# An attention and expert layer on one core: a new order of the step, with the combine weights spread by DMA

## The chip, the cores and the metric

One core of a Trainium2 chip runs the whole layer. The metric is device time in microseconds from the start to the end of one execution.

## The reference

Sixteen sequences ("batches" below) of 256 tokens with 128 features pass through attention and then an expert layer, each with a residual:

```python
x = x + attn(layernorm(x), Wqg, Wkv, Wout)
x = x + ffn(layernorm(x), ...)
# attn, per head (16 heads, 16 key and 64 value features)
q, k, v = l2norm(q), l2norm(k), l2norm(v)
attn = square(relu(q @ k.T)); aggr = attn @ v
out = tanh(norm(aggr)) * aggr / norm(aggr) * tanh(silu(gates)) @ Wout
# ffn, 16 routed experts (4 chosen per token, group limited) and one shared
inter = silu(x @ w_gate[e]) * (x @ w_up[e])
y = sum_e combine[:, e] * (inter[e] @ w_down[e]) + shared
```

`combine` holds the four chosen scores of a token, normed to a sum of 2.5, and zeros.

## The kernel before

The work is a software pipeline over batches. In step s (from -2 to 18) six stages run side by side on different batches: `L` (batch s+2: layer norm, transposed `xT`, projections `qk` and `v`), `P` (s+1: gate projection `g`, norms of q, k, v), `A` (s: scores, relu, square, values of 16 heads), `O` (s-1: head norms, output projection `y`, residual, second layer norm, `x2T`), `F` (s-2: router `lg`, nine gate and up projections `gu`, combine weights), `D` (s-3: down projection `y2`). Steps 2 to 15 hold `F` within the general plan; steps 16 and 17 have end plans of their own.

A step has eight slots. In each, TensorE runs the fillers that `FILL` lists for the slot, then the scores of the next pair of heads, then the values of this pair (`values` of slot k end the slot). Every engine follows this order in its own queue: ScalarE reads PSUM (relu, silu, squares, copies), GpSimd squares the relus into `p` (L363), and VectorE's list is written out by hand in its `step`, slot by slot. Fillers take the four PSUM banks `ps_f` in turn, so job n of a step waits until job n-4 has been read (`wait_for_bank`).

Names that matter: `scale_hidden` (L920) multiplies the hidden values `it` by the combine weights of two experts' columns; these stand in PSUM, where `cT` (transposes) and `cB` 0 to 3 (matmuls with the selection matrix `sel`, L454) spread them over the partitions. `rT` and `rB` do the same for head scales, read by `scale_heads` (L911). `gate_up` (L903) multiplies silu and up projection, reading the bank of a `gu`. `gated_heads` (L949) multiplies the values by the gates. `head_norm_roots` runs the Newton rounds for inverse roots (L696 to L698), `route_scores`, `route_groups` and `route_experts` choose the experts. `low_parts`, `sums`, `low_rows` and `output_rows` are VectorE's readers of `qk`, `v`'s squares, `x2T` and `y2`. GpSimd also scales the values by their norms (L381), in slots 4 to 7.

SyncE (SP) issues all DMAs from one queue, in this order in a step: store of the output, load of `x_res`, load of `x_in`, store of the q and k parts to DRAM (`qk_rows`, 1 MB), and twelve loads back in another layout (`qkt`, 2 MB), which are wanted at the end of the next step.

## Time and profile before

| | |
|---|---|
| median of three runs | 714.83 us (712.07 to 715.86) |
| the profiled execution | 712.51 us, of which the span of instructions 710.5 us |
| mean granted TensorE clock | 0.99 |
| TensorE busy | 665.4 us (94%) |
| VectorE, ScalarE, GpSimd busy | 478.0, 431.8, 352.1 us |
| DMA queue of SP | 60.26 MB, 57.3% of 16 engines |

TensorE's busy share is from modelled ends of pipelined matmuls; the distance between the starts of two jobs is the better measure of what a job takes. A bracket behind a timeline row gives idle time before it and what ended it. Times of a row count from the start of the span.

### The profile page before, as it was taken

The page shows a single profiled execution, that of the slowest core. Times are in us where ns is not written, and L with a number is a line of the kernel's source. Part 1 is how long each engine was busy: PE and PEld are TensorE (multiplying, and loading weights), DVE is VectorE, ACT ScalarE, POOL GpSimd, SP SyncE. Part 2 cuts the span into 40 slices and gives each one's busy share as a digit, 9 for nine tenths or more (in the row PEclk, how much of TensorE's full clock was granted, in tenths as well). Part 3 has the DMA queues.
Part 4 walks back from the last instruction along what each step waited for, and adds up shares of the span by engine and source line. Part 5 has one row for each costly group of instructions (what it writes and reads, how often), then busy time and mean ns, then how long its engine had stood idle before and what let it go on. Part 6 is the DMA issues. An engine that isn't in the chain of part 4 may idle for free.

```text
span 710.5 us, 15317 instructions
## 1 busy us (share of the span) xinstructions
PE 665.4 (94%) x5160; PEld 515.8 (73%) x5160; DVE 478.0 (67%) x1771; ACT 431.8 (61%) x986; POOL 352.1 (50%) x368
## 2 busy tenths in 40 slices
PE   3689899999999999999999999999999999999977
PEld 2455567787787777778777778778777877767677
DVE  5745558676767777676767767576876767566684
ACT  3768576756566766656676775656667565644312
POOL 3348574645546464645555564555546355464200
PEclk9899999999999999999999999999999999999999
DMA  9998948290937639191855819094672909300000
GB/s 254 136 142 137 119 103 103 78 117 28 138 46 125 77 91 104 62 124 26 134 68 102 100 61 133 10 144 58 113 81 78 113 27 136 37 16 2 8 1 16
DMA packets 72829, 61.24 MB, mean 86 GB/s; under 512 B 8624, under 2 KB 72496, under 8 KB 72752
## 3 DMA queue, kind: packets, MB, share of 16 engines
q1 hardware_dynamic: 72752, 60.26, 57.3%
q8 instruction: 42, 0.69, 0.5%
q14 instruction: 35, 0.29, 0.1%
HBM read 41.37 MB, written 18.87 MB: 85 GB/s over the span
## 4 chain that ended last, share of the span: by engine, by line
PE 69%; ACT 12%; DVE 9%; issue 7%; POOL 2%; DMA 1%; SPq 0%; DVEq 0%; ACTq 0%; POOLq 0%
PE ps_a L539 14%; PE ps_f L395 10%; PE ps_f L479 9%; PE ps_f L458 8%; PE ps_f L396 7%; PE ps_f L397 7%; PE ps_s L507 5%; ACT sq L605 3%; PE ps_f L437 3%; ACT v L602 3%; ACT r L641 3%; DVE it L920 2%; POOL p L363 2%; PE ps_f L454 2%; DVE big L911 2%
## 5 line engine op out<-in xcount | busy, mean ns | idle before, releaser
L363 POOL TENSOR_TENSOR p<-r 128x512 f32<-128x512 f32 x256 | 260.8, 1040 | 288.7 <-ACT r L641 253.5
L641 ACT ACTIVATE r<-ps_s 128x512 f32<-128x512 f32 x256 | 142.3, 621 | 84.3 <-PE ps_s L507 79.0
L539 PE MATMUL ps_a<-p,v 128*64 128x256 f32 x1024 | 147.1, 393 | 3.5 <-POOL p L363 2.5
L539 PEld LDWEIGHTS ps_a<-p,v 128*64 128x64 f32 x1024 | 64.7, 136 | 45.3 <-POOL p L363 7.7
L633 ACT ACTIVATE it<-ps_f 128x256 f32<-128x256 f32 x144 | 55.2, 383 | 65.3 <-PE ps_f L397 54.4
L949 DVE TENSOR_TENSOR big<-ps_a,wt 128x256 f32<-128x256 f32 x128 | 54.1, 422 | 58.9 <-ACT big L650 57.2
L903 DVE TENSOR_TENSOR it<-ps_f,it 128x256 f32<-128x256 f32 x144 | 58.3, 421 | 42.3 <-ACT it L633 41.2
L479 PE MATMUL ps_f<-wdown,it 128*128 128x128 f32 x576 | 69.4, 280 | 2.8 <-DVE it L920 2.8
L479 PEld LDWEIGHTS ps_f<-wdown,it 128*128 128x128 f32 x576 | 66.8, 195 | 4.2 <-DVE it L920 3.8
L381 POOL TENSOR_TENSOR v<-v,vs 128x512 f32<-128x512 f32 x64 | 67.7, 1060 | 3.5 <-DVE vs L821 3.5
L650 ACT ACTIVATE big<-ps_a 128x256 f32<-128x256 f32 x128 | 53.5, 418 | 25.5 <-PE ps_f L437 22.9
L507 PE MATMUL ps_s<-qkt 64*128 64x256 f32 x512 | 65.3, 330 | 1.4 <-ACT r L641 1.1
L458 PEld LDWEIGHTS ps_f<-wout,big 128*128 128x128 f32 x512 | 59.5, 192 | 6.6 <-issue 5.8
L458 PE MATMUL ps_f<-wout,big 128*128 128x128 f32 x512 | 63.5, 278 | 0.7 <-DVE big L911 0.7
L611 ACT ACTIVATE wt<-ps_f 128x512 f32<-128x512 f32 x64 | 38.3, 598 | 31.6 <-PE ps_f L397 30.1
L507 PEld LDWEIGHTS ps_s<-qkt 64*128 64x128 f32 x512 | 38.6, 184 | 24.1 <-issue 10.9
L787 DVE TENSOR_REDUCE norms_m<-sq 128x8 f32<-128x512 f32 x64 | 43.7, 683 | 15.0 <-ACT sq L605 15.0
L780 DVE TENSOR_TENSOR qk_parts<-ps_f,qk_parts 128x512 fp32r<-128x512 f32 x32 | 22.0, 691 | 41.4 <-ACT qk_sq L597 41.4
L395 PE MATMUL ps_f<-x2h,weg_hi 128*128 128x256 f32 x144 | 46.9, 326 | 2.3 <-DVE o_sb L928 1.3
L911 DVE TENSOR_TENSOR big<-ps_f,big 128x512 f32<-128x512 f32 x64 | 42.4, 685 | 5.7 <-PE ps_f L454 5.6
L602 ACT ACTIVATE v<-ps_f 128x512 f32<-128x512 f32 x64 | 42.2, 659 | 4.3 <-DVE sel L768 2.2
L920 DVE TENSOR_TENSOR it<-ps_f,it 128x512 f32<-128x512 f32 x64 | 43.4, 684 | 0.5
(154 smaller groups left out, 1444.5 us busy)
## 6 DMA issues: line engine op xcount, KB each, us to landing
qk_rows<-qk_parts SPq DMA_DIRECT2D x16, 1024.0 KB, 4.5
qkt<-qk_rows SPq DMA_DIRECT2D x64, 256.0 KB, 9.6
qkt<-qk_rows SPq DMA_DIRECT2D x128, 128.0 KB, 9.0
x_in<-in_L_attn_tokens SPq DMA_DIRECT2D x16, 128.0 KB, 2.2
x_res<-in_L_attn_tokens SPq DMA_DIRECT2D x16, 128.0 KB, 13.6
out<-o_sb SPq DMA_DIRECT2D x16, 128.0 KB, 13.6
big<-in_L_attn_Wqg SPq DMA_DIRECT2D x1, 640.0 KB, 4.1
big<-in_L_attn_Wkv SPq DMA_DIRECT2D x1, 640.0 KB, 5.3
```

What stands on the lines that cost most here:

```text
L363: pool.tensor_tensor(p[h % 4][:], r[h % 2][:], r[h % 2][:], ALU.mult).then_inc(probs_done, 1)
L381: pool.tensor_tensor(view, view, broadcast(scale, [P, NP, DV], 2), ALU.mult)\
L395: pe.matmul(dst, stat[0], mov[0], start=True, stop=False)
L458: last = pe.matmul(ps[:, 0:D], aw[pb][:, c, tok[j]], wout[:, c, :], start=(c == 0), stop=(c == NP - 1))
L479: last = pe.matmul(ps[:, 0:D], it[:, c, tok[j]], wdown[:, c, :], start=(c == 0), stop=(c == FC - 1))
L507: last = pe.matmul(ps_s[e][:, t * N:(t + 1) * N], qkt[q][rows, 1, k, t * P:(t + 1) * P], qkt[q][rows, 0, k, :], start=True, stop=True)
L539: last = pe.matmul(ps_a[64 * e:64 * e + 64, 0:N], v[s % 3][:, t, h * DV:(h + 1) * DV], p[h % 4][:, t * N:(t + 1) * N], start=(t == 0), sto ...
L602: act.activation(v[b % 3][:, j // 2, (j % 2) * 512:(j % 2 + 1) * 512], ps[:], ACT.Copy)
L641: act.activation(r[h % 2][:], ps_s[h % 2][:], ACT.Relu).then_inc(relu_done, 1)
L903: dve.tensor_tensor(it[:, c, :], bank[("gu", c)][:, N:2 * N], it[:, c, :], ALU.mult)\
L911: dve.tensor_tensor(part, bank[("rB", j)][:].rearrange("p (c n) -> p c n", n=N), part, ALU.mult)\
L920: dve.tensor_tensor(part, bank[("cB", j)][:].rearrange("p (c n) -> p c n", n=N), part, ALU.mult).then_inc(read["cB"], 1)
```

## The change

- `FILL` is new: `cB` and `cT` leave it, `cD` (two transposes of the 16 combine weights) comes in; `v` 3 moves to slot 0 of the next step (stage `P`); the two halves of `y2` stand in slots 0 and 1; `gu` runs in slots 2 to 7.
- For the 14 batches whose `F` is in steps 2 to 15 (`BY_DMA`), ScalarE copies `cD` to `ctr`, SP stores it to DRAM and loads it back broadcast over 64 partitions for each of two halves (`cb`, 1 MB), and GpSimd multiplies `it` by `cb` in slots 5 to 7. VectorE's `scale_hidden` stays for the last two batches only.
- GpSimd scales the first half of the values in slot 4 and the second in slots 0 and 1 of the next step.
- VectorE's list follows: the Newton rounds are in slot 1, `route_experts` in slot 2, `sums` 2 and 3 in slot 0 of the next step.
- Gates and gated heads share three rotating buffers (`heads3`) in place of `wt` and `aw`; gates are multiplied in place.

The core of the diff (left out: the same renaming in other places, semaphores, counts by `nth`):

```diff
 
     SKIP = ("-", "skip", 0)
     FILL = [
-        [("F", "lg", 0), ("D", "y2", 0), ("D", "y2", 1)],
-        [("N", "ones", 0), ("F", "gu", 0), ("P", "g", 0), ("N", "nT", 0), ("F", "gu", 1)],
-        [("F", "gu", 2), ("P", "g", 1), ("F", "gu", 3), ("F", "gu", 4)],
-        [("P", "g", 2), ("F", "gu", 5), ("F", "cT", 0), ("F", "gu", 6), ("O", "rT", 0)],
-        [("O", "rB", 0), ("O", "rB", 1), ("F", "gu", 7), ("O", "rB", 2), ("L", "xT", 0), ("O", "rB", 3), ("P", "g", 3),
-         ("F", "gu", 8)],
-        [("O", "y", 0), ("L", "qk", 0), ("O", "y", 1), ("F", "cB", 0)],
-        [("L", "qk", 1), ("L", "v", 0), ("F", "cB", 1), ("L", "v", 1), SKIP],
-        [("L", "v", 2), ("F", "cB", 2), ("L", "v", 3), ("F", "cB", 3), ("O", "x2T", 0), SKIP],
+        [("F", "lg", 0), ("P", "v", 3), ("D", "y2", 0), ("N", "ones", 0)],
+        [("N", "nT", 0), ("D", "y2", 1), ("P", "g", 0)],
+        [("F", "gu", 0), ("F", "gu", 1), ("P", "g", 1), ("F", "gu", 2)],
+        [("F", "gu", 3), ("F", "cD", 0), ("P", "g", 2), ("O", "rT", 0), ("F", "gu", 4)],
+        [("O", "rB", 0), ("O", "rB", 1), ("F", "gu", 5), ("O", "rB", 2), ("L", "xT", 0), ("O", "rB", 3), ("P", "g", 3)],
+        [("O", "y", 0), ("O", "y", 1), ("L", "qk", 0)],
+        [("F", "gu", 6), ("L", "qk", 1), ("L", "v", 0), ("F", "gu", 7)],
+        [("L", "v", 1), ("F", "gu", 8), ("O", "x2T", 0), ("L", "v", 2), SKIP, SKIP],
     ]
     ENDS = {
         B: [
...
     assert all(len(plan) == SLOTS and sum(len(slot) for slot in plan) % 4 == 0 for plan in (FILL, *ENDS.values()))
     OFFSET = {"L": 2, "P": 1, "N": 1, "A": 0, "O": -1, "F": -2, "D": -3}
     JOBS = {"xT": 1, "qk": 2, "v": 4, "g": 4, "ones": 1, "nT": 1, "rT": 1, "rB": 4, "y": 2,
-            "x2T": 1, "lg": 1, "gu": FC, "cT": 1, "cB": 4, "y2": 2}
+            "x2T": 1, "lg": 1, "gu": FC, "cD": 1, "cT": 1, "cB": 4, "y2": 2}
+    BY_DMA = B - 2
+
+    def nth(kind, b):
+        return b - BY_DMA if kind in ("cT", "cB") else b
 
     def stages(s):
...
+
+        big = sb("big", [P, 4 * NP * N])
         a2 = big[:, 0:NP * N].rearrange("p (c n) -> p c n", n=N)
-        aw = [big[:, q * NP * N:(q + 1) * NP * N].rearrange("p (c n) -> p c n", n=N) for q in (1, 2)]
-        raw_experts = 3 * NP * N - 2 * FC * P
-        assert 2 * (HK + HV) <= raw_experts and 2 * NP * N - N <= raw_experts
+        heads3 = [big[:, m * NP * N:(m + 1) * NP * N].rearrange("p (c n) -> p c n", n=N) for m in (1, 2, 3)]
+        raw_experts = 4 * NP * N - 2 * FC * P
+        assert 2 * (HK + HV) <= 2 * NP * N <= raw_experts
 
         x_in = [sb(f"x_in{q}", [P, T, D]) for q in range(2)]
...
                             sp.dma_start(dst[:, 0], rows[lq, 0, e]).then_inc(qk_loaded[q], 16)
                             sp.dma_start(dst[:, 1], rows[lk, 1, e]).then_inc(qk_loaded[q], 16)
 
+            def spread_combine(b):
+
+                sp.wait_ge(read["cD"], b + 1)
+                wait(sp, c_spread, 32 * b)
+                sp.dma_start(c_rows.rearrange("e (c n) -> (e c) n", n=N), ctr[:]).then_inc(c_stored, 16)
+                sp.wait_ge(c_stored, 16 * b + 16)
+                wait(sp, it_scaled, 4 * b)
+                for e in range(2):
+                    sp.dma_start(cb[64 * e:64 * e + 64, :, :].rearrange("p c n -> p (c n)"),
+                                 c_rows[e:e + 1, :].broadcast_to([64, NP * N])).then_inc(c_spread, 16)
+
             def step(s, q, on, at):
 
                 if "D" in on:
...
                 if "A" in on:
                     wait(sp, read["y"], 2 * (s - 1))
                     sp.dma_start(x_res[q][:], tokens[s].rearrange("(t p) d -> p t d", p=P)).then_inc(x_back[q], 16)
+                if "F" in on and at < B:
+                    spread_combine(s - 2)
                 if "L" in on:
                     b = s + 2
...
+            def scale_values(b, half, ts):
+
+                pool.wait_ge(vs_ready, b + 1)
+                pool.wait_ge(read["v"], 4 * b + 4)
+                for t in ts:
+                    view = v[b % 3][:, t, half * 512:(half + 1) * 512].rearrange("p (h d) -> p h d", d=DV)
+                    scale = vs[:, t, half * NP:(half + 1) * NP]
+                    pool.tensor_tensor(view, view, broadcast(scale, [P, NP, DV], 2), ALU.mult).then_inc(v_normed, 1)
+
             def step(s, q, on, at):
                 for k in range(SLOTS):
                     if "A" in on:
...
                         root(rstd1, var1, rstd1_ready)
                     if k == 1 and at == FIRST_STEP:
                         tables()
+                    if "P" in on and k == 4:
+                        scale_values(s + 1, 0, (0, 1))
+                    if "A" in on and k in (0, 1):
+                        scale_values(s, 1, (k,))
                     if k == 6 and "O" in on:
                         pool.wait_ge(ch_n, 3 * s)
                         root(rstd2, var2, rstd2_ready)
-                    if "P" in on:
-                        b = s + 1
-                        if k in (4, 5, 6, 7):
-
-                            t, half = divmod(k - 4, 2)
-                            pool.wait_ge(vs_ready, b + 1)
-                            pool.wait_ge(read["v"], 4 * b + k - 3)
-                            view = v[b % 3][:, t, half * 512:(half + 1) * 512].rearrange("p (h d) -> p h d", d=DV)
-                            scale = vs[:, t, half * NP:(half + 1) * NP]
-                            pool.tensor_tensor(view, view, broadcast(scale, [P, NP, DV], 2), ALU.mult)\
-                                .then_inc(v_normed, 1)
+                    if "F" in on and at < B and k in (5, 6, 7):
+                        b = s - 2
+                        for j in ((0, 1), (2,), (3,))[k - 5]:
+                            pool.wait_ge(read["gu"], FC * b + 2 * j + 2)
+                            pool.wait_ge(c_spread, 32 * b + 32)
+                            part = it[:, 2 * j:2 * j + 2, :]
+                            pool.tensor_tensor(part, part, cb[:, 2 * j:2 * j + 2, :], ALU.mult).then_inc(it_scaled, 1)
 
             run_flat(step)
 
...
                     three(ps[:, 0:N], (weg[0][:, cols], weg[1][:, cols]), (x2h[:], x2l[:]))
                     last = three(ps[:, N:2 * N], (weu[0][:, cols], weu[1][:, cols]), (x2h[:], x2l[:]))
                 else:
-                    pe.wait_ge(read["cB"], 4 * b + 4)
+                    if b < BY_DMA:
+                        pe.wait_ge(it_scaled, 4 * b + 4)
+                    else:
...
                         wait(pe, aw_done, 8 * s + k)
-                        if k == 0:
-                            pe.wait_ge(v_normed, 4 * s + 4)
+                        if k in (0, 4):
+                            pe.wait_ge(v_normed, 4 * s + (2 if k == 0 else 4))
                         for t in range(T):
...
                     act.activation(squares_at(j), ps[:], ACT.Square).then_inc(read[kind], 1)
                 elif kind == "g":
                     if j == 0:
-                        wait(act, aw_done, 8 * (b - 1))
+                        wait(act, done["y"], 2 * (b - 2))
                     act.wait_ge(done[kind], count)
-                    dst = wt[pq][:, 2 * j:2 * j + 2, :]
+                    dst = heads3[b % 3][:, 2 * j:2 * j + 2, :]
                     act.activation(dst, ps[:].rearrange("p (c n) -> p c n", n=N), ACT.Silu).then_inc(read[kind], 1)
                 elif kind == "ones":
...
                     act.wait_ge(done[kind], count)
                     act.activation(spread[0:2 * H, :], ps[0:2 * H, 0:N], ACT.Copy).then_inc(read[kind], 1)
+                elif kind == "cD":
+                    wait(act, c_stored, 16 * b)
+                    act.wait_ge(done[kind], count)
+                    act.activation(ctr[:], ps[0:E, 0:N], ACT.Copy).then_inc(read[kind], 1)
                 elif kind == "x2T":
                     wait(act, done["gu"], FC * b)
...
                             value_weights()
-                        if (kind, j) == ("gu", 0 if at == B else 4) and "O" in on:
+                        if (kind, j) == ("gu", 0) and "O" in on:
                             act.wait_ge(n_ready, s)
...
                 link(dve.tensor_reduce(den, chosen[:], AX.X, ALU.add))
                 link(dve.tensor_scalar(den, den, 1e-20, None, ALU.add))
                 link(dve.reciprocal(den, den))
+                if b < BY_DMA:
+                    wait(dve, done["cD"], b)
+                    for t in range(T):
+                        last = dve.scalar_tensor_tensor(out=comb_rows[:, t, :].rearrange("p (e c) -> p c e", e=2),
+                                                        in0=chosen[:, t, :].rearrange("p (c e) -> p c e", e=2), scalar=SCALE,
+                                                        in1=broadcast(den[:, t:t + 1], [P, EC, 2], 2), op0=ALU.mult,
+                                                        op1=ALU.mult)
+                    last.then_inc(c_ready, 1)
+                    return
                 link(dve.scalar_tensor_tensor(out=comb, in0=chosen[:], scalar=SCALE,
                                               in1=broadcast(den, [P, T, E], 2), op0=ALU.mult, op1=ALU.mult))
                 split(link, cs, comb, c_ready)
...
 
                 def head_norm_roots():
                     norms_start(link_norms, P_on, O, s)
                     newton(link_norms)
                     if at < B:
-                        gated_heads(2)
+                        gated_heads(1)
                     newton(link_norms)
                     newton(link_norms)
 
...
                 for k in range(SLOTS):
                     if k == 0:
                         gated_heads(k)
+                        if P_on:
+                            sums(2, s + 1)
                         if F:
                             route_scores(link_f, fb)
+                            route_groups(link_f)
+                        if P_on:
+                            sums(3, s + 1)
                         if L_on:
                             dve.wait_ge(x_loaded[q], (s + 2 - q) * 8 + 16)
                             row_stats(link_l, x_in[q], st1, mv1, var1)
                             link_l.end()
-                        if F:
-                            route_groups(link_f)
                         if "D" in on:
-                            output_rows()
+                            output_rows([0])
                     if k == 1:
-                        if F:
-                            route_experts(link_f, fb)
-                            link_f.end()
+                        if P_on or O:
+                            head_sums(P_on, O, s)
+                            head_norm_roots()
+                        if O:
+                            head_norms(link_o, b, rq2[pq])
+                        if "D" in on:
+                            output_rows([1])
+                    if k == 2:
                         gated_heads(k)
                         if F:
                             gate_up([0])
-                        if P_on or O:
-                            head_sums(P_on, O, s)
-                        if F:
+                            route_experts(link_f, fb)
+                            link_f.end()
                             gate_up([1])
-                    if k == 2:
-                        if P_on or O:
-                            head_norm_roots()
-                        if O:
-                            head_norms(link_o, b, rq2[pq])
-                        if F:
-                            gate_up([2])
-                        if F:
-                            gate_up([3, 4])
-                    if k == 3:
                         if O:
                             head_scales(link_o, b)
                             link_o.end()
+                        if F:
+                            gate_up([2])
+                    if k == 3:
                         gated_heads(k)
                         if F:
-                            gate_up([5])
+                            gate_up([3])
                         if P_on:
                             value_scales(link_p, s + 1, rq2[pq])
...
                         if at == FIRST_STEP:
                             query_key_weights()
                         if F:
-                            gate_up([6])
+                            gate_up([4])
                     if k == 4:
                         if O:
                             scale_heads([0, 1])
+                        if F:
+                            gate_up([5])
                         gated_heads(k)
-                        if F:
-                            gate_up([7])
                         if O:
                             scale_heads([2])
                         if L_on:
...
                                .then_inc(read["xT"], 1)
                         if O:
                             scale_heads([3])
-                        if F:
-                            gate_up([8])
                     if k == 5:
                         gated_heads(k)
                         if at == -1:
...
                         if O:
                             dve.wait_ge(x_back[pq], (b - pq) * 8 + 16)
                             residual_row(0)
-                        if L_on:
-                            low_parts(0, s + 2)
-                        if O:
                             residual_row(1)
                             dve.wait_ge(read["y"], 2 * b + 2)
                             row_stats(link_n, x1[pq], st2, mv2, var2)
                             link_n.end()
-                        if F:
-                            scale_hidden([0])
+                        if L_on:
+                            low_parts(0, s + 2)
                     if k == 6:
                         gated_heads(k)
+                        if F:
+                            gate_up([6])
                         if L_on:
                             low_parts(1, s + 2)
                         if at == FIRST_STEP:
                             value_weights()
                         if L_on:
                             sums(0, s + 2)
-                        if F:
-                            scale_hidden([1])
                         if O:
                             second_norm()
+                        if F:
+                            gate_up([7])
+                    if k == 7:
+                        gated_heads(k)
+                        if F:
+                            gate_up([8])
                         if L_on:
                             sums(1, s + 2)
-                    if k == 7:
-                        gated_heads(k)
-                        if L_on:
-                            sums(2, s + 2)
-                        if F:
-                            scale_hidden([2])
-                        if L_on:
-                            sums(3, s + 2)
-                        if F:
-                            scale_hidden([3])
                         if O:
                             low_rows()
 
```

## Rows read from the trace of the kernel before

**Rows 1.** The page, part 1: busy time of each engine, share of the span, instructions.
```profile
PE 665.4 (94%) x5160; PEld 515.8 (73%) x5160; DVE 478.0 (67%) x1771; ACT 431.8 (61%) x986; POOL 352.1 (50%) x368
```

**Rows 2.** The page, part 4: the chain of waits, its shares by engine.
```profile
PE 69%; ACT 12%; DVE 9%; issue 7%; POOL 2%; DMA 1%; SPq 0%; DVEq 0%; ACTq 0%; POOLq 0%
```

**Rows 3.** TensorE's timeline: start us, us, engine, line, operation; first `lg` of steps 3, 14, 15, 16.
```profile
140.30 0.62 PE L467 MATMUL ps_f<-wroute,xn 128*128 128x16 f32 x4
...
589.46 0.62 PE L467 MATMUL ps_f<-wroute,xn 128*128 128x16 f32 x4
...
627.99 0.62 PE L467 MATMUL ps_f<-wroute,xn 128*128 128x16 f32 x4
...
662.67 0.62 PE L467 MATMUL ps_f<-wroute,xn 128*128 128x16 f32 x4
```

**Rows 4.** TensorE's timeline around its waits; in brackets idle time before and its releaser.
```profile
367.17 0.51 PE L454 MATMUL ps_f<-rt,sel 128*128 128x256 f32 x2
367.83 0.39 PE L395 MATMUL ps_f<-xh,wg_hi 128*128 128x256 f32 x1 [0.16 <-DVE it L903]
...
382.77 0.39 PE L454 MATMUL ps_f<-ct,sel 128*128 128x256 f32 x2
383.49 0.44 PE L463 MATMUL ps_f<-ident,xn 128*128 128x128 f32 x2 [0.32 <-ACT sq L605]
...
385.30 0.62 PE L467 MATMUL ps_f<-wroute,xn 128*128 128x16 f32 x4
386.09 4.26 PE L479 MATMUL ps_f<-wdown,it 128*128 128x128 f32 x36 [0.17 <-DVE it L920]
```

**Rows 5.** TensorE's timeline, one steady step: jobs by the distance between starts.
```profile
378.58 0.40 PE L454 MATMUL ps_f<-ct,sel 128*128 128x256 f32 x2
378.82 0.39 PE L395 MATMUL ps_f<-wv_hi,xh 128*128 128x512 f32 x1
...
390.27 0.50 PE L507 MATMUL ps_s<-qkt 64*128 64x256 f32 x4
...
391.72 1.07 PE L437 MATMUL ps_f<-big,ones 128*32 128x256 f32 x16
...
393.15 0.38 PE L395 MATMUL ps_f<-x2h,weg_hi 128*128 128x256 f32 x1
...
394.68 0.54 PE L442 MATMUL ps_f<-pick,n2row 128*128 128x48 f32 x4
```

**Rows 6.** Groups by line and shape: busy us, mean ns of one, idle before.
```profile
L363 POOL TENSOR_TENSOR p<-r 128x512 f32<-128x512 f32 x256 | 260.8, 1040 | 288.7 <-ACT r L641 253.5 <-PE ps_a L539 35.1
...
L920 DVE TENSOR_TENSOR it<-ps_f,it 128x512 f32<-128x512 f32 x64 | 43.4, 684 | 0.5
```

**Rows 7.** VectorE's timeline: first operation of the expert choice, norm chain in the tail.
```profile
390.60 0.18 DVE L877 MAX8 top<-cand 128x8 f32<-128x24 f32 x1
...
667.07 0.19 DVE L796 COPY norms_m<-ps_f 128x32 f32<-128x32 f32 x1 [2.51 <-PE ps_f L442]
...
670.70 0.29 DVE L928 TENSOR_TENSOR o_sb<-ps_f,x 128x128 f32<-128x128 f32 x1
```

**Rows 8.** Windows of a steady step: engines' busy us, granted clock, DMA share, GB/s.
```profile
399.30:401.30 2.00, 2.00 (x19) 1.65 (x19) 1.83 (x9) 1.54 (x5) 0.01 (x1) 1.00 1.15 111
...
403.30:405.30 2.00, 2.00 (x19) 1.63 (x19) 1.20 (x5) 1.59 (x6) 0.94 (x1) 1.00 0.25 66
...
sum 42.00, PE 41.18 PEld 32.50 DVE 30.00 ACT 27.48 POOL 22.49; mean PE 1.96 PEld 1.55 DVE 1.43 ACT 1.31 POOL 1.07
```

**Rows 9.** SP's timeline of DMA issues, then issues by line with time to landing.
```profile
384.44 0.33 SPq L287 DMA_DIRECT2D qkt<-qk_rows  x1
...
391.14 0.46 SPq L300 DMA_DIRECT2D x_res<-in_L_attn_tokens  x1
...
qk_rows<-qk_parts SPq DMA_DIRECT2D x16, 1024.0 KB, 4.5
...
x_res<-in_L_attn_tokens SPq DMA_DIRECT2D x16, 128.0 KB, 13.6
```

37 lines of the change are left out of this document (20 added, 17 removed).

## The prediction

> **What bounds the kernel now.** I read the engine totals first: TensorE is busy 665.4 of 710.5 us, VectorE, ScalarE and GpSimd 478, 432 and 352 [rows 1]. The chain of waits agrees: 69% of it is TensorE, 12% ScalarE, 9% VectorE, 7% issue [rows 2]. Next I asked for TensorE's timeline and marked the first matmul of `lg`, which opens each step. Steps 3 to 13 repeat to a hundredth: 140.30 to 589.46 is eleven steps of 40.83 us. Step 14 takes 38.53, step 15 34.68, and what follows 662.67 belongs to the two end plans [rows 3]. Before 140.30 lie loading, the partly filled steps -2 to 1, and step 2, a steady one without `y2`. The granted clock is 1.00 throughout a steady step, the higher of the two levels [rows 8].
>
> Inside a steady step the listed idle stretches of TensorE are only 0.16 us in slot 4, 0.32 in slot 7 and 0.17 in slot 0 [rows 4], the same three in every steady step. The modelled ends hide a bit more; distances between starts show it. `rB` 3 starts at 367.17 and `g` 3 at 367.83, where a pair of `sel` matmuls takes 0.24 elsewhere: 0.42 us of waiting for `it` L903. `cB` 3 starts at 382.77 and `x2T` at 383.49: 0.48 of waiting for the squares. `lg` to `y2` is 0.79 where four short matmuls take about 0.5: 0.3 waiting for the last `scale_hidden` (L920) [rows 4, 5]. So the step is 39.6 us of TensorE work and 1.2 us of waiting. The other engines matter only through such waits.
>
> **The change part by part.** Times are counted from a step's start T0 (its `lg`).
>
> 1. *`cB` goes from TensorE.* Four pairs of matmuls, each start to start 0.24 us (378.58 to 378.82) [rows 5]: 0.96 us a step, all on the bound engine, in steps 2 to 15. `cT` becomes `cD`, two transposes as before, 0.22 either way. Certain.
>
> 2. *The waits.* The 0.3 at `y2` goes if the GpSimd scaling of parts 2 and 3 ends in time. The 0.48 at `x2T` was a PSUM bank whose reader was the second `v` of slot 7; now the bank belongs to `v` 0, read much earlier: gone. The 0.42 at `g` 3 stays possible. What is late next I looked for by walking the queues with durations of rows: on TensorE, start to start: `y2` 2.1 each (386.09 to 390.27 for 36 matmuls), so `y` with 32 for the two 1.85 each; scores plus values 1.45 (390.27 to 391.72), `ones` 1.43 (to 393.15), `gu` plus `g`, twelve matmuls of 256 columns, 1.53 (to 394.68), so each of these and `qk` 0.72 to 0.8, and `v`, three of 512 columns, 0.7; transposes and `nT` 0.2 to 0.4 [rows 4, 5]. The new slots are then 6.2, 4.7, 4.5, 4.2, 4.4, 5.95, 4.45 and 4.2 us: 38.6, which is also 40.83 - 0.96 - 1.2.
>  - Slot 0: `y2` 0 is due at T0+1.2. GpSimd has p14 and p15 in slot 7 (1.04 each [rows 6]), then part 3 of `it`, ending about T0-0.6. Slack 1.8. `lg` now waits for `low_rows`, since its bank was `x2T`'s: that ends, after `gate_up` 8 and one `sums`, about 0.2 before T0. Thin.
>  - Slots 1 and 2: the norm chain (head sums, seed, three Newton rounds, norms) takes 4.5 us of VectorE (667.07 to 670.70 in the tail's uncovered copy, plus a gated head and one output row) [rows 7]. It starts 0.5 into slot 1 and ends as slot 2 begins; `route_experts`, thirteen small operations of 0.18 as the first of them [rows 7], 2.4 us, less one, follows behind `gate_up` 0. `cD` gets its input about 0.9 before its turn, `rT` about 1.3 before. Queued behind it all are `gate_up` 1 to 3; `gu` 4 needs the bank of `gu` 3, free only 0.2 before. Thin.
>  - Slot 4: `g` 3 needs `gate_up` 5 and waits about 0.15.
>  - Slot 5: `qk` 0 now ends the slot, so ScalarE does copy, square and a tanh (0.5 each) ahead of the relus of heads 12 and 13. Those end 1.1 into slot 6, GpSimd's squares 2.7 into it, and values 6 are due at 3.4. Slack 0.6.
>  I take 0.4 us of new waits, a third of today's, because the thin places are of the size of the error of such a walk. Bounds: 0 and 1.6 (all three thin places plus what they cost each other).
>
> 3. *GpSimd.* It gains four multiplications of 128x512, priced by its own 1.04 [rows 6]: 4.2 us a step, on 22.5 busy of 42 [rows 8]. VectorE loses four of 0.68 [rows 6] and two small ones. The two value scalings moved to slots 0 and 1 cost nothing while slot 0's 6.2 covers 3 x 1.04, and slot 1's 4.7 covers 2 x 1.04 + 0.69 + 1.04. The halves are waited for at slots 0 and 4, both long past.
>
> 4. *The DMAs.* `spread_combine` stands on SP before the next `x_in` and the `qk` store. SP's queue decides when it can land. `qkt` loads are issued from 384.44, 0.86 before T0, and the last small transfer behind them (`x_res`, issued 391.14) lands 13.7 later; the DMA share falls from 1.15 at T0+14 to 0.25 at T0+18 [rows 8, 9]. So the rings are full until about T0+18.5 and free from there to the next `qk` store, in slot 6. `ctr` is copied at about T0+17.2. Its store of 16 KB goes behind the backlog and lands near T0+20.3; the two loads (1 MB in all) follow. At the rate of the `qk` store, 1024 KB in 4.5 us from issue to landing [rows 9], they land at T0+25.5; at the rate of the `qkt` loads, 111 GB/s in the first window and 116 from the first issue to the last landing (2.36 MB in 20.4 us) [rows 8, 9], they take 8.7 and some 1.5 of latency and land at T0+30.5. I take T0+26.5, nearer the store, because the new rows are 8 KB long on 64 partitions and the `qkt` pieces 1 KB on 16. GpSimd needs them before parts 0 and 1, behind which p12 and p13 are queued. Values 6 are due at T0+33.4, so p12 must start by 31.2 and part 0 by 29.1. That is the deadline: 2.6 us of slack, and a microsecond per step for each microsecond beyond. The next `x_in` goes behind the loads and is wanted in the next step's slot 0, over 10 us later: nothing. The output store and `x_res` go out some 6 us later: nothing.
>  The Trainium skill has a rule that speaks against these loads. "SBUF — State Buffer", section "Door 1: The DMA port swizzle", says that a range of 64 partitions reaches only 8 of the 16 DMA ports. With its 436 GB/s for all ports that is an estimate of 2.4 us per half, and with the 2.0 fixed of "DMA: Bandwidth & Descriptors" both land near T0+27.1: still hidden, with 2.0 of slack. The same rule gives 16 partitions at most 4 ports, about 109 GB/s, and the trace's 111 to 116 with the `qkt` loads is near it; by the rule, then, the slow rate belongs to those loads' shape and not to the new ones.
>
> 5. *One buffer for gates and heads.* `wt` and `aw` become three rotating buffers. The product is in place, same form, 0.42 us. The gates of batch s+1 wait for `y` of s-2, done a step ago. Nothing.
>
> 6. *The other steps.* Step 2 has no `y2`, so slot 1 is only 2.6 us and the norm chain sticks out: of the 1.8 us of a steady step it keeps 1.0. Step 14 loses the `L` jobs; today it has 34.9 us of TensorE work (39.6 less `xT` 0.4, `qk` 1.5 and `v` 2.8) in 38.53 [rows 3], since slots 6 and 7 are nearly empty of fillers and each head waits for relu and square. Now it has 34.6 (`v` 3 stays), `gu` 6 to 8 stand in those slots, and GpSimd has 10.1 us there and in slot 5 against 10.9 of TensorE: I take 1.4 of waits, 36.0, gain 2.5 (bounds 0.3 and 3.9). Step 15 the same with `g` gone: 30.9 of work, about 2.1 of waits for `gate_up` and GpSimd, 33.0 against 34.68, gain 1.7. Steps -2 to 1 only shift `v` 3 and the Newton rounds by a slot; bounds -1 and +1, one `v` and one Newton round (0.7 each [rows 5, 7]) with a wait; I take 0. The end plans keep `cT` and `cB`: 0.
>
> **Sum.** Steady period 38.6 + 0.4 = 39.0, gain 1.83 x 11 = 20.1; plus 1.0 + 2.5 + 1.7 = 25.3. The profiled execution took 712.5 (span 710.5): it becomes 687.2. The median of the runs shown is 2.3 above it: 714.8 becomes 689.5.
>
> **The rivals.**
>  *A, the forecast* (680 to 697): waits between 0 and 0.9 us a step. 2.23 x 11 + 7.5 = 32 gives 683; with the start up to 1 us better and rounding, 680. For it: TensorE is dense and 0.96 us is certain.
>  *B, the freed waits come back elsewhere*: `gu` 4, `g` 3 and `lg` all wait as VectorE's order is tight, 1.6 us in the step. Period 40.2, gain 0.63 x 11 = 7, plus 3 of the odd steps: 705; the case spans 697 to 710. For it: today's step holds waits of just this kind at 0.3 to 0.5 each. Against: VectorE sheds 3 us.
>  *C, the spread comes late, slower*: the mechanism is GpSimd waiting in slot 5 for `c_spread` with p12 and p13 queued behind. At the `qkt` rate, T0+30.5, it costs 1.4 a step: period 40.4, about 707, no loss yet. It turns into a loss once landing is over 1.83 + 0.5 past the deadline, T0+31.4, which is a rate below some 110 GB/s. At 90 GB/s (11.7 + 1.5 behind T0+20.3) landing is T0+33.5: 4.4 late, period 43.4, +2.6 x 14: 751. For it: 64 reads of the same 8 KB, which no row shows, and the slow `qkt` rows. Against: the store's rate.
>  *D, it doesn't do what it says*: the norm rounds or the part of `y2` move a wait of the same size and `cB` was filling time in which TensorE would have waited anyway, so nothing: 712 to 718. Against: TensorE's timeline shows `cB` back to back with its neighbours.
>
> **How the numbers follow.** A 0.62, B 0.17 (of it 0.15 faster), C 0.16 (0.03 faster, 0.01 same, 0.12 slower), D 0.05 (0.04 same, 0.01 slower). About 0.5%, 3.6 us, is what a measurement of this kernel can tell from no change. Faster 0.80, same 0.07, slower 0.13. The forecast is A's, 689.5. The range leaves out C's slow part and D's upper half, and a little below A: 680 to 712.
>
> **What would show it.** Steady period near 39.0 between two `lg`; slots 6.2 and 4.7 for 0 and 1. Step 1 of the change: no `ct`,`sel` pair before the end plans. Step 2: idle before `x2T` gone, idle before `g` 3 or `gu` 4 of 0.1 to 0.3. Step 4: `cb` lands 6 us after its issue, and GpSimd's first `it` multiplication starts at about T0+26.5 without p12 moving. Wrong if the first `it` multiplication starts after T0+29, if TensorE lists idle over 1 us a step, or if relus 12 and 13 end later than 1.5 into slot 6.

## The result, and the profile after

| | before | after |
|---|---|---|
| median of four runs | 714.6 us (712.07 to 715.86) | 687.73 us (687.0 to 688.13) |
| profiled execution, its span | 712.51, 710.5 us | 687.0, 685.3 us |
| ratio of times, 95% interval | | 0.9633 (0.9612 to 0.9654) |

The kernel became 3.7% faster. The page after, parts 1 and 4, answers to [rows 1] and [rows 2]:

```profile
PE 646.5 (94%) x5048; PEld 501.7 (73%) x5048; DVE 446.9 (65%) x1701; ACT 427.7 (62%) x986; POOL 420.2 (61%) x424
...
PE 84%; DVE 5%; ACT 5%; issue 3%; POOL 2%; DMA 1%; SPq 0%; DVEq 0%; ACTq 0%; POOLq 0%
```

TensorE lost 18.9 us of work, GpSimd gained 68.1 and VectorE lost 31.1. The chain of waits is now 84% TensorE where it was 69%: fewer waits of other engines stand in it. TensorE's timeline at the first `lg` of steps 2, 3, 14, 15 and 16 answers to [rows 3]:

```profile
100.78 0.62 PE L497 MATMUL ps_f<-wroute,xn 128*128 128x16 f32 x4
...
139.73 0.62 PE L497 MATMUL ps_f<-wroute,xn 128*128 128x16 f32 x4
...
567.26 0.62 PE L497 MATMUL ps_f<-wroute,xn 128*128 128x16 f32 x4
...
605.58 0.62 PE L497 MATMUL ps_f<-wroute,xn 128*128 128x16 f32 x4
...
638.96 0.62 PE L497 MATMUL ps_f<-wroute,xn 128*128 128x16 f32 x4
```

Eleven steps from 139.73 to 567.26 are 38.87 us each, against 40.83. All the stretches, in us:

| stretch | before | after | difference | predicted |
|---|---|---|---|---|
| start of the span to `lg` of step 2 | 102.49 | 100.78 | -1.71 | 0 |
| step 2 | 37.81 | 38.95 | +1.14 | -1.0 |
| steps 3 to 13 | 449.16 | 427.53 | -21.6 | -20.1 |
| step 14 | 38.53 | 38.32 | -0.21 | -2.5 |
| step 15 | 34.68 | 33.38 | -1.30 | -1.7 |
| `lg` of step 16 to the end | 47.83 | 46.34 | -1.49 | 0 |
| span | 710.5 | 685.3 | -25.2 | -25.3 |

The sum agrees better than its terms. This is one steady step on TensorE (T0 = 372.93; rows at the starts of `lg`, slots 1 and 2, `cD`, `rB` 3, `g` 3, slot 6, `x2T` and the next `lg`):

```profile
372.93 0.62 PE L497 MATMUL ps_f<-wroute,xn 128*128 128x16 f32 x4
...
379.15 0.65 PE L468 MATMUL ps_f<-pick,n2row 128*128 128x48 f32 x4
...
383.95 0.39 PE L421 MATMUL ps_f<-x2h,weg_hi 128*128 128x256 f32 x1
...
389.26 0.38 PE L478 MATMUL ps_f<-ident,comb_rows 128*16 128x128 f32 x2
...
394.58 0.50 PE L484 MATMUL ps_f<-rt,sel 128*128 128x256 f32 x2
395.08 0.39 PE L421 MATMUL ps_f<-xh,wg_hi 128*128 128x256 f32 x1
...
403.36 0.39 PE L421 MATMUL ps_f<-x2h,weg_hi 128*128 128x256 f32 x1
...
409.34 0.38 PE L493 MATMUL ps_f<-ident,xn 128*128 128x128 f32 x2
...
411.79 0.62 PE L497 MATMUL ps_f<-wroute,xn 128*128 128x16 f32 x4
```

No row of the step has a bracket: the three waits of [rows 4] are gone, and no new one is listed. Slots 0 to 7 last 6.22, 4.80, 4.49, 4.25, 4.74, 5.93, 4.47 and 3.96 us. What is hidden lies in slot 4, where `rB` 3 to `g` 3 takes 0.50 and a pair takes 0.24: 0.26 us of waiting for `gate_up` 5.

The spread of the combine weights in the same step: SP's timeline (store, then the two loads), and GpSimd's, where the two multiplications by `cb` are followed by p12 and p13:

```profile
390.13 0.33 SPq L300 DMA_DIRECT2D c_rows<-ctr  x1
394.41 1.09 SPq L304 DMA_DIRECT2D cb<-c_rows  x2
```

```profile
401.80 2.53 POOL L408 TENSOR_TENSOR it<-it,cb 128x512 f32<-128x512 f32 x2 [1.93 <-DMA cb<-c_rows]
404.31 2.04 POOL L389 TENSOR_TENSOR p<-r 128x512 f32<-128x512 f32 x2
```

The store goes out at T0+17.2, the loads at T0+21.5, and GpSimd starts at T0+28.9, having waited 1.93 for the loads. p12, the square of head 12's relus, starts at T0+31.4 and TensorE waits for nothing. Over steps 2 to 14 the loads are issued between T0+20.2 and T0+22.3, and the first multiplication starts between T0+27.5 and T0+29.3; the period of steps 3 to 13 is 38.87 all the same.

Three odd places. **Step 2**, TensorE's timeline and the windows around its wait (busy us by engine, granted clock, DMA share, GB/s):

```profile
109.30 1.94 PE L572 MATMUL ps_a<-p,v 128*64 128x256 f32 x8 [2.34 <-DVE big L994]
```

```profile
107.00:109.00 2.00, 0.00 (x0) 0.00 (x0) 1.69 (x9) 1.20 (x3) 1.90 (x4) 1.00 1.15 110
109.00:111.00 2.00, 1.71 (x8) 0.75 (x8) 1.76 (x9) 0.00 (x0) 1.81 (x2) 0.59 1.16 114
111.00:113.00 2.00, 2.00 (x11) 1.83 (x10) 0.64 (x3) 0.53 (x2) 0.00 (x0) 0.55 1.16 116
```

Values 1 wait 2.34 us for `gated_heads(1)` (L994), which stands on VectorE behind the head sums and the first Newton round; with no `y2` in slot 1 nothing covers it. Then the granted clock reads 0.59 and 0.55 in two windows, near the 1.2 GHz level: eight value matmuls take 1.87 us from start to start and not 1.02, and the window from 111 holds 11 matmuls where a steady one holds 19. That is 0.85 + 2 x 8/19 = 1.7 us on top of the wait.

**Step 14**, TensorE's timeline: values 6 and 7 wait for GpSimd, whose multiplications wait for the loads until T0+28.9 in a step whose slots 6 and 7 lack the `L` jobs. In four of the kernels below GpSimd has the same list in this step, and there as in after the step ends 9.46 to 9.48 us after GpSimd's first multiplication: 28.86 and 38.32 here, 28.37 and 37.83 in pairs_back, 27.43 and 36.89 in v3_back. With early data the step takes 36.61 (spread_once, below), and by the same 9.46 that puts the deadline of step 14 at T0+27.2.

```profile
599.78 0.62 PE L572 MATMUL ps_a<-p,v 128*64 128x256 f32 x2 [0.69 <-POOL p L389]
...
603.67 0.62 PE L572 MATMUL ps_a<-p,v 128*64 128x256 f32 x2 [0.34 <-POOL p L389]
```

**The tail.** One execution of before has a lull and then a stretch at the lower clock, that of after has the same lull and keeps the higher clock. Windows of before, then of after:

```profile
684.00:686.00 2.00, 0.49 (x5) 0.32 (x4) 1.74 (x6) 0.38 (x1) 0.65 (x1) 1.00 0.00 0
...
690.00:692.00 2.00, 2.00 (x11) 2.00 (x11) 1.71 (x13) 0.00 (x0) 0.00 (x0) 0.50 0.03 8
```

```profile
660.00:662.00 2.00, 0.70 (x6) 0.50 (x5) 1.64 (x7) 0.56 (x2) 0.69 (x1) 1.00 0.00 0
...
666.00:668.00 2.00, 2.00 (x20) 2.00 (x19) 1.75 (x15) 0.00 (x0) 0.00 (x0) 1.00 0.00 0
```

At 0.50 TensorE starts 11 matmuls in 2 us, at 1.00 it starts 20. With the 0.74 and 0.90 of the neighbouring windows that is about 1.7 us of clock, about what the last stretch differs by (1.49): an event of this one execution, not of the change. The fourteen profiled executions of this document bear it out. From the `lg` of step 17 to the end, which is the same work in all but narrow_cb, the two with 1.00 there (after, both_ends) take 20.8 us, four take 22.2 to 22.3 (before among them), and eight take 23.0 to 23.8.

The start can't be read so. From 20 to 50 us before has 0.84, 0.82 and 0.83 in its windows of 10 us and after has 1.00, but spread_once, whose start is the same program as that of after, has 0.83, 0.66 and 0.83 and takes 100.79 us to the `lg` of step 2, where after takes 100.78. Six kernels with this same start take 99.6 to 101.0, three of them with the lower clock there and three without. The two with the start of before take 102.5 and 104.4 (narrow_cb), and v3_back takes 103.7. So the 1.71 us are rather the order, perhaps the move of `v` 3, than the clock; one execution of each doesn't show it, and y2_together, with `v` 3 moved, takes 103.2.

So about 1.5 of the 25.2 us of the profiled pair are clock and not order; 21.6 come from the eleven steady steps. The medians differ by 26.9, and can't be split so: only the profiled executions have windows. The four runs of after have mean clocks of 0.980 to 0.998, so others have falls too.

### The profile page after: what moved, and what is told of

It reads as the page before. It is cut to its first block, busy times and chain, and to the rows that moved or that the text cites. A ratio compares the mean times of both kernels' runs of the same rounds, so it can differ in the third digit from the quotient of the medians.

```text
span 685.3 us, 15157 instructions
## 1 busy us (share of the span) xinstructions
PE 646.5 (94%) x5048; PEld 501.7 (73%) x5048; DVE 446.9 (65%) x1701; ACT 427.7 (62%) x986; POOL 420.2 (61%) x424
## 4 chain that ended last, share of the span: by engine, by line
PE 84%; DVE 5%; ACT 5%; issue 3%; POOL 2%; DMA 1%; SPq 0%; DVEq 0%; ACTq 0%; POOLq 0%
PE ps_a L572 18%; PE ps_f L421 13%; PE ps_f L422 10%; PE ps_f L423 10%; PE ps_f L488 9%; PE ps_f L512 9%; PE ps_s L540 7%; PE ps_f L463 3%; PE ps_f L484 3%; POOL p L389 2%; PE ps_f L468 1%; PE ps_f L497 1%; DMA big<-in_L_attn_Wkv 1%; ACT r L678 1%; ACT sq L638 1%
## 5 line engine op out<-in xcount | busy, mean ns | idle before, releaser
L389 POOL TENSOR_TENSOR p<-r 128x512 f32<-128x512 f32 x256 | 260.9, 1040 | 177.5 <-ACT r L678 108.9
L572 PE MATMUL ps_a<-p,v 128*64 128x256 f32 x1024 | 145.5, 394 | 9.4 <-DVE big L994 4.7
L678 ACT ACTIVATE r<-ps_s 128x512 f32<-128x512 f32 x256 | 140.7, 613 | 13.5 <-PE ps_s L540 10.6
L994 DVE TENSOR_TENSOR big<-ps_a,big 128x256 f32<-128x256 f32 x128 | 54.1, 423 | 77.8 <-ACT big L687 77.2
L408 POOL TENSOR_TENSOR it<-it,cb 128x512 f32<-128x512 f32 x56 | 71.2, 1282 | 18.9 <-DMA cb<-c_rows 18.8
L644 ACT ACTIVATE big<-ps_f 128x512 f32<-128x512 f32 x64 | 38.2, 598 | 66.2 <-PE ps_f L423 66.2
L949 DVE TENSOR_TENSOR it<-ps_f,it 128x256 f32<-128x256 f32 x144 | 60.6, 421 | 27.7 <-ACT it L670 26.5
L380 POOL TENSOR_TENSOR v<-v,vs 128x512 f32<-128x512 f32 x64 | 66.1, 1043 | 3.5 <-DVE vs L858 3.5
L488 PE MATMUL ps_f<-wout,big 128*128 128x128 f32 x512 | 61.4, 278 | 0.8 <-DVE big L957 0.8
L628 ACT ACTIVATE qk_parts<-ps_f 128x512 fp32r<-128x512 f32 x32 | 19.2, 599 | 51.8 <-PE ps_f L423 51.7
L371 POOL TENSOR_TENSOR rstd<-var,minus_half 128x2 f32<-128x2 f32 x32 | 22.1, 689 | 39.2 <-DVE var L747 39.1
```

Of the source, the lines that this page charges most:

```text
L380: pool.tensor_tensor(view, view, broadcast(scale, [P, NP, DV], 2), ALU.mult).then_inc(v_normed, 1)
L389: pool.tensor_tensor(p[h % 4][:], r[h % 2][:], r[h % 2][:], ALU.mult).then_inc(probs_done, 1)
L408: pool.tensor_tensor(part, part, cb[:, 2 * j:2 * j + 2, :], ALU.mult).then_inc(it_scaled, 1)
L488: last = pe.matmul(ps[:, 0:D], heads3[b % 3][:, c, tok[j]], wout[:, c, :], start=(c == 0), stop=(c == NP - 1))
L572: last = pe.matmul(ps_a[64 * e:64 * e + 64, 0:N], v[s % 3][:, t, h * DV:(h + 1) * DV], p[h % 4][:, t * N:(t + 1) * N], start=(t == 0), sto ...
L678: act.activation(r[h % 2][:], ps_s[h % 2][:], ACT.Relu).then_inc(relu_done, 1)
```

## The experiments

Theory T, from the prediction: the gain is the work of `cB` plus the waits that the new order removes, the spread is hidden, and it has a deadline at T0+29.1 beyond which each microsecond costs one. Rivals: the pairs were filling time that TensorE would have waited (D), the waits come back (B), the spread costs (C). Ratios are to the kernel before, run on the same chip; "period" is the distance of two `lg` in steady steps, 40.83 before and 38.87 after. The edits are shown shortened: semaphores and line breaks are left out, and `...` stands for arguments that stay.

| kernel | median us | ratio (95%) | period |
|---|---|---|---|
| narrow_cb | 711.29 | 0.9969 (0.9953 to 0.9984) | 40.70 |
| pairs_back | 699.80 | 0.9805 (0.9778 to 0.9832) | 39.86 |
| y2_together | 722.91 | 1.0137 (1.0114 to 1.0160) | 41.28, two of 42.8 |
| newton_back | 700.73 | 0.9811 (0.9787 to 0.9835) | 39.86 |
| v3_back | 688.79 | 0.9641 (0.9618 to 0.9663) | 38.87 |
| v_scales_back | 698.01 | 0.9771 (0.9743 to 0.9800) | 39.57 |
| spread_once | 687.27 | 0.9627 (0.9609 to 0.9645) | 38.88 |
| spread_more | 697.56 | 0.9754 (0.9702 to 0.9807) | 38.87 to 40.41 |
| scale_on_dve | 695.71 | 0.9741 (0.9717 to 0.9765) | 39.52 |
| one_stream | 687.09, one run | | 38.88, one of 39.40 |
| heads_first | 687.38 | 0.9630 (0.9605 to 0.9654) | 38.88 |
| both_ends | 685.82 | 0.9603 (0.9578 to 0.9627) | 38.88, one of 39.71 |

### The pairs of `cB`: narrow_cb and pairs_back

narrow_cb is the kernel before with `cB` of 8 columns and not 256:

```diff
-  pe.matmul(ps[:, c * N:(c + 1) * N], sel[...], spread[:], ...)
+  wide = N if kind == "rB" else 8
+  pe.matmul(ps[:, c * N:c * N + wide], sel[...], spread[:, 0:wide], ...)
```

> The kernel before, with the cB matmuls cut from 256 to 8 columns; banks, waits and readers stay, and the hidden values are scaled by whatever the bank holds, so the output is not the layer's. Theory (the matmul work of cB is worth its own time on TensorE, the waits are apart from it): a pair falls from 0.24 us to about 0.12 (two weight loads), 0.12 x 4 pairs x 14 steps = 6.7 us at most; since the waits before x2T and y2 stay or grow, 708 to 712 us. Rival D (cB filled time in which TensorE would have waited anyway): no change, 714 to 716 us, with the idle before x2T and y2 grown by what was cut.

The period fell by 0.13 us. A pair now takes 0.14 from start to start and not 0.24, but not all of that was cut from TensorE's work. TensorE's timeline of before, then of narrow_cb, at `cB` 0, the scores behind it and `qk` 1:

```profile
375.22 0.48 PE L454 MATMUL ps_f<-ct,sel 128*128 128x256 f32 x2
375.63 0.50 PE L507 MATMUL ps_s<-qkt 64*128 64x256 f32 x4
...
377.07 0.39 PE L395 MATMUL ps_f<-xh,wqk_hi 128*128 128x256 f32 x1
```

```profile
376.38 0.36 PE L455 MATMUL ps_f<-ct,sel 128*128 128x8 f32 x2
376.67 0.51 PE L508 MATMUL ps_s<-qkt 64*128 64x256 f32 x4
...
378.12 0.39 PE L395 MATMUL ps_f<-xh,wqk_hi 128*128 128x256 f32 x1
```

and of narrow_cb at `cB` 3 and `x2T`:

```profile
383.82 0.28 PE L455 MATMUL ps_f<-ct,sel 128*128 128x8 f32 x2
384.54 0.44 PE L464 MATMUL ps_f<-ident,xn 128*128 128x128 f32 x2 [0.43 <-ACT sq L606]
```

`cB` 0 gave 0.12 (0.41 to 0.29 up to the scores), which is all of the gain. `cB` 1 and 2 gave nothing: behind the narrow pair the first matmul of the next `v` takes 0.31 and not 0.23, so that pair and matmul together take 0.45 to 0.47 in both kernels. Behind `cB` 3 the idle time grew from 0.32 to 0.43, and from the pair to `x2T` it is 0.72 us, as in [rows 4] (382.77 to 383.49).

Nor would more have come if the three pairs had been cut whole, as far as ScalarE's timeline of before shows: its first reading of `qk` 1 and the square of `v` 2, for which `x2T` waits:

```profile
378.15 0.60 ACT L595 ACTIVATE qk_parts<-ps_f 128x512 fp32r<-128x512 f32 x1 [0.57 <-PE ps_f L397]
...
382.72 0.71 ACT L605 ACTIVATE sq<-ps_f 128x512 f32<-128x512 f32 x1
```

Between them ScalarE has no idle time, and from `qk` 1 to `x2T` it is 6.42 us in both kernels (377.07 to 383.49, 378.12 to 384.54). That distance is ScalarE's. In the order before, `cB` 1 to 3 stood inside it, as rival D said; only `cB` 0 was work that could be saved.

pairs_back is the kernel after with four idle pairs put back into slots 5 to 7:

```diff
+  if "F" in on and at < B and (kind, j) in (("qk", 0), ("v", 0), ("v", 1), ("v", 2)):
+      for c in range(2):
+          pe.matmul(ps[:, c * N:(c + 1) * N], sel[:, 2 * j + c, :], <sel>, start=True, stop=True)
```

> The changed kernel with four pairs of matmuls of cB's size put back on TensorE (into banks that the next job overwrites) in slots 5, 6, 7 and 7, in the 12 steps that have stage L. Theory: each costs its 0.24 us start to start, 0.96 a step, 12 steps: +11.5 us, 699 us. Rival: the changed step waits in those slots for GpSimd or ScalarE, and the pairs hide there: 688 to 692 us.

The period grew by 0.99, four times 0.25, with no bracket in the step. In the new order the pairs would cost their full length. Half of the gain of a step, 0.99 of 1.96, is thus the pairs' work, but only given the new order; in the old one `cB` 0's quarter of it was to be had. The other half is the order's, and is there with idle pairs on TensorE too (699.80 us).

### The order: y2_together, newton_back, v3_back, v_scales_back

y2_together moves one tuple, `y2` 1, back to slot 0:

```diff
-  [..., ("D", "y2", 0), ("N", "ones", 0)],
-  [("N", "nT", 0), ("D", "y2", 1), ("P", "g", 0)],
+  [..., ("D", "y2", 0), ("D", "y2", 1), ("N", "ones", 0)],
+  [("N", "nT", 0), ("P", "g", 0)],
```

> The changed kernel with both halves of y2 in slot 0 and slot 1 left with nT and g 0 only. Theory: y2 1 covers VectorE's norm chain in slot 1 (3.9 us from the head sums to nn, as in step 2, where slot 1 has no y2 and the values waited 2.34 us); without it 1.0 to 1.8 us a step come back in 13 steps: 701 to 711 us. Rival: the order of y2 is neutral, since slot 0 gains what slot 1 loses and VectorE has more time ahead: 687 to 690 us.

It is slower than the kernel before, and 2.4 us a step slower than after, where I expected 1.0 to 1.8. TensorE's timeline in the step from 391.15, and a window behind it:

```profile
402.27 1.08 PE L572 MATMUL ps_a<-p,v 128*64 128x256 f32 x8 [1.03 <-DVE big L994]
404.58 0.39 PE L421 MATMUL ps_f<-x2h,weg_hi 128*128 128x256 f32 x1 [1.23 <-DVE o_sb L974]
```

```profile
405.00:407.00 2.00, 2.00 (x11) 2.00 (x11) 0.51 (x4) 0.50 (x2) 0.00 (x0) 0.50 1.14 129
```

With 2.1 us less in slot 1, `gated_heads(1)` inside the Newton rounds holds values 1 (1.03), the output row holds the next filler's bank (1.23), and in two of eleven steps the clock falls to 0.50 behind them; those take 42.8 and not 41.3. The step before has the same two waits (1.04 and 1.21) and 1.00 in the windows behind them. It is what step 2 of the kernel after shows, in every step: parting `y2` is what makes the early Newton rounds possible.

newton_back puts them into slot 2 again, and the tanh of the head norms behind `gu` 2:

```diff
                     if k == 1:
+                        gated_heads(k)
                         head_sums(P_on, O, s)
-                        head_norm_roots()
-                        head_norms(link_o, b, rq2[pq])
                         output_rows([1])
                     if k == 2:
+                        head_norm_roots()
+                        head_norms(link_o, b, rq2[pq])
```

> The changed kernel with the Newton rounds and head norms in slot 2 of VectorE's list instead of slot 1 (the head sums stay in slot 1, the tanh of the norms goes behind gu 2). Theory: now the combine weights are ready 1.7 us and the head scales 1.5 us ahead of their transposes in slot 3; the chain of 3.3 us behind them in slot 2 makes both late by about 1.8 us, so TensorE waits at cD and rT in 14 steps: +20 to +30 us, 708 to 718 us. Rival: the VectorE idle in slots 1 and 2 absorbs it and the round's place is worth nothing: 687 to 690 us.

The period grew by 1.0: waits of 0.37 at `cD` and 0.22 at the `gu` behind `rT`, the rest hidden. TensorE's timeline (`it` of L949 is `gate_up`, which follows the late expert choice in VectorE's list):

```profile
395.02 0.39 PE L478 MATMUL ps_f<-ident,comb_rows 128*16 128x128 f32 x2 [0.37 <-DVE it L949]
...
396.57 0.39 PE L421 MATMUL ps_f<-x2h,weg_hi 128*128 128x256 f32 x1 [0.22 <-DVE it L949]
```

The chain that I called thin is thin, but a slot of delay costs half of what I expected of it.

v3_back returns `v` 3 and its sums to slot 7 of the step before:

```diff
-  [("F", "lg", 0), ("P", "v", 3), ("D", "y2", 0), ("N", "ones", 0)],
+  [("F", "lg", 0), ("D", "y2", 0), ("N", "ones", 0)],
-  [..., ("O", "x2T", 0), ("L", "v", 2), SKIP, SKIP],
+  [..., ("O", "x2T", 0), ("L", "v", 2), ("L", "v", 3), SKIP, SKIP],
```

> The changed kernel with v 3 at the end of slot 7, as before the change, and VectorE's sums 2 and 3 with it. TensorE's work in the step is the same. Theory (ScalarE's copy and square of v 3, 1.0 us, then stand ahead of the relus of the next heads and of x2T's reader; slot 0 has 5.5 us to absorb it): 0 to 0.5 us a step, 688 to 695 us. Rival (the move was needed as relus 0 and 1 come late): over 1 us a step, 700 us and more.

The period is 38.87 as after: in steady steps this move is worth nothing. v_scales_back puts all value scalings back into slots 4 to 7 of GpSimd:

```diff
-                    if "P" in on and k == 4:
-                        scale_values(s + 1, 0, (0, 1))
-                    if "A" in on and k in (0, 1):
-                        scale_values(s, 1, (k,))
+                    if "P" in on and k >= 4:
+                        scale_values(s + 1, (k - 4) // 2, ((k - 4) % 2,))
```

> The changed kernel with the four value scalings on GpSimd in slots 4 to 7, one each, as before the change. Slots 5 to 7 then hold three more of 1.04 us; behind the wait for the spread (T0+27.5 to 29.3) stand parts 0 and 1, a scaling and p12, p13, which end at T0+34 to 35.9 where values 6 are due at 33.9. Theory: 1 to 3 us a step in 11 steps, 699 to 720 us. Rival (GpSimd's idle of 2.5 us per slot absorbs them): 687 to 690 us.

+0.70 a step. 0.5 of it lies in values 7, which take 1.5 us from start to start and not 1.0: a scaling and the multiplication of part 2 then stand ahead of p14 and p15. The move is needed, but its price is below the 1 to 3 us that I expected.

### The spread: spread_once and spread_more

spread_once issues the two loads in step 2 only; the later batches are scaled with that batch's weights.

```diff
-                wait(sp, c_spread, 32 * b)
-                for e in range(2):
+                wait(sp, c_spread, 32 if b else 0)
+                for e in range(2) if b == 0 else ():
```

> The changed kernel with the two broadcast loads made once, in step 2, and left out in the 13 later steps (the stores stay), so later batches are scaled by the first one's weights. In the changed kernel GpSimd's first it multiplication waits 1 to 2.3 us for the loads in 13 steps, and they land 28.7 us into the step, 0.4 before the deadline worked out beforehand (29.1). Theory (the wait is hidden; below the deadline the landing is worth nothing): 687 to 688.5 us, period 38.8 to 38.9. Rival C in small (the spread already holds TensorE back at times): 680 to 685 us.

The period stays at 38.88, so thirteen spreads of 1 MB cost no steady step anything. Step 14 takes 36.61 and not 38.32: there the late landing costs 1.7 us.

spread_more puts 512 KB of other traffic ahead of the loads, to find the deadline:

```diff
+                sp.dma_start(cb2, c_rows[0:1, :].broadcast_to([64, NP * N])).then_inc(c_more, 16)
                 for e in range(2):
                     sp.dma_start(cb[64 * e:64 * e + 64, ...], ...)
```

> The changed kernel with one more 512 KB broadcast, into DRAM, issued ahead of the two loads in each of the 14 steps. It should put their landing 2 to 3 us later, to T0+31 to 32. Theory (deadline at T0+29.1 and a microsecond for each one beyond): 1.9 to 2.9 us a step, +27 to +40 us, 714 to 728 us. Rival (GpSimd catches up before values 6 and more slack is hidden, or the extra traffic runs beside): under 1 us a step, 688 to 700 us.

The landing moved by about 1.2 us only and not by 2 to 3, which is why the time is far below the 714 us and more that I expected. But it scatters from step to step, and that gives the price. GpSimd's timeline in steps 5 and 8 (T0 = 219.63 and 337.80):

```profile
250.46 2.56 POOL L413 TENSOR_TENSOR it<-it,cb 128x512 f32<-128x512 f32 x2 [3.88 <-DMA cb<-c_rows]
...
368.09 2.54 POOL L413 TENSOR_TENSOR it<-it,cb 128x512 f32<-128x512 f32 x2 [3.34 <-DMA cb<-c_rows]
```

| first multiplication, T0+ | up to 29.26 | 29.43 | 29.87 | 30.14 | 30.29 | 30.78 | 30.83 |
|---|---|---|---|---|---|---|---|
| period | 38.87 to 38.89 | 39.01 | 39.44 | 39.71 | 39.85 | 40.35 | 40.41 |

Each point is 38.87 + (x - 29.3) within 0.03. The deadline in steady steps is T0+29.3 (predicted 29.1) and the price a microsecond for a microsecond. The profiled execution of after has its latest at 29.31: the deadline is just met. In both_ends, below, one steady step has 30.13 and takes 39.71, and the rule gives 39.70.

### Who multiplies: scale_on_dve and one_stream

scale_on_dve gives the multiplications by `cb` to VectorE, as before, with `cb` still from the DMA:

```diff
+                def scale_by_cb(js):
+                    for j in js:
+                        part = it[:, 2 * j:2 * j + 2, :]
+                        dve.tensor_tensor(part, part, cb[:, 2 * j:2 * j + 2, :], ALU.mult)
```

> The changed kernel with the multiplications by cb on VectorE (slots 5 to 7, 128x512 from SBUF) instead of GpSimd, in steps 2 to 15. VectorE then has 2.7 us more, GpSimd 5.1 less. Theory (TensorE bounds the steady step, either engine hides the work; steps 14 and 15, where GpSimd bounds, gain 1 to 3 us together): 684 to 688 us. Rival (VectorE's list in slots 6 and 7 is the tight one, so low_rows and gate_up come late): 0.3 to 1 us a step, 691 to 702 us.

The period grew by 0.65. VectorE's timeline, beside a busy GpSimd and beside an idle one:

```profile
408.37 2.13 DVE L975 TENSOR_TENSOR it<-it,cb 128x512 f32<-128x512 f32 x2
...
416.13 0.68 DVE L975 TENSOR_TENSOR it<-it,cb 128x512 f32<-128x512 f32 x1
```

GpSimd's squares beside the first of these (two undisturbed ones are the row 404.31 of after, above):

```profile
408.81 2.59 POOL L389 TENSOR_TENSOR p<-r 128x512 f32<-128x512 f32 x2 [4.44 <-ACT r L678]
```

The second operation of each pair, VectorE's, then GpSimd's:

```profile
408.97 1.53 DVE L975 TENSOR_TENSOR it<-it,cb 128x512 f32<-128x512 f32 x1
```

```profile
409.91 1.49 POOL L389 TENSOR_TENSOR p<-r 128x512 f32<-128x512 f32 x1
```

Alone a multiplication takes 0.68. Beside GpSimd's squares the pair takes 2.13, and it is the second that pays: begun just after GpSimd's first square, it takes 1.53, the longest of 56, and ends at 410.50. GpSimd's second square takes 1.49 and not 1.04. With `ps_f` as second operand the same operation took 0.684 [rows 6]. The two engines hold each other up when VectorE reads both operands from SBUF. The Trainium skill, "SBUF — State Buffer", section "SBUF: two separate sides", has the rule: a VectorE operation with two SBUF inputs and a GpSimd operation that reads SBUF lock each other out of a shared pair of ports. The rows agree: VectorE's 1.53 is what is left of GpSimd's square (to about 409.85) and then 0.65 of its own.

TensorE loses the time where VectorE's list has become late, as the rival had it. Its timeline at `v` 2, behind `x2T` at 414.00:

```profile
414.59 0.50 PE L421 MATMUL ps_f<-wv_hi,xh 128*128 128x512 f32 x1 [0.21 <-DVE it L949]
```

`v` 2 waits for `gate_up` 7, which stands behind the multiplication of part 2: it starts 0.59 after `x2T`, where after has 0.14 (409.34 to 409.48). How much of the 0.65 is the lock and how much the 2.7 us more that VectorE has to do, no run separates.

one_stream asks why GpSimd takes 1282 ns and not the 1040 of [rows 6] that I charged. Its second operand is the first again, so the combine weights are left out:

```diff
-  pool.tensor_tensor(part, part, cb[:, 2 * j:2 * j + 2, :], ALU.mult)
+  pool.tensor_tensor(part, part, part, ALU.mult)
```

> The changed kernel with the hidden values multiplied by themselves instead of by cb on GpSimd, so the combine weights are left out; waits and places stay. In the changed kernel this operation takes 1282 ns (1266 to 1297 over 56), where relu times itself and values times a broadcast scale take 1040. Theory (two full, different SBUF streams are what costs the extra 240 ns): 1040 ns. Rival (another engine's access at the same time, or the place in the step): still about 1280 ns. The time of the kernel: 687 to 688 us under both, as GpSimd is not the bound in a steady step.

Groups by line and shape, one_stream and then after:

```profile
L408 POOL TENSOR_TENSOR it<-it 128x512 f32<-128x512 f32 x56 | 57.8, 1042 | 21.1 <-DMA cb<-c_rows 21.1
```

```profile
L408 POOL TENSOR_TENSOR it<-it,cb 128x512 f32<-128x512 f32 x56 | 71.2, 1282 | 18.9 <-DMA cb<-c_rows 18.8
```

1042 with one tensor read, 1282 with two. Four such operations a step are 0.96 us more on GpSimd than priced. Ten of eleven steady periods do not show it (38.88). The eleventh is 39.40, with a first multiplication at T0+30.32. That is 0.53 more than 38.87, and with the two multiplications ahead of p12 cheaper by 0.48 the deadline of T0+29.3 becomes 29.8: the rule holds here too. Steps 14 and 15 show the price itself: 36.38 and 33.14, where spread_once, whose data is also there in time, has 36.61 and 33.38.

### Mending the odd steps: heads_first and both_ends

heads_first puts `gated_heads(1)` ahead of the head sums in steps without `D`, against the wait of step 2:

```diff
+                        if "D" not in on:
+                            gated_heads(1)
                         if P_on or O:
                             head_sums(P_on, O, s)
```

> The changed kernel with gated_heads 1 ahead of the head sums in the steps without stage D (up to step 2), where slot 1 is short; there the values of pair 1 waited 1.25, 1.11 and 2.34 us for VectorE, since gated_heads 1 stands inside the Newton rounds. Theory: 3 to 4.5 us in all, 683 to 685 us. Rival (the norm chain then ends 0.4 us later in each of these steps and TensorE waits for it at rT or gu 4 instead): 0 to 1.5 us, 686 to 688 us.

Step 2 became 1.65 us shorter (38.95 to 37.30), from a wait shorter by 1.73 and a clock that stays at 1.00. TensorE's timeline there:

```profile
107.44 1.08 PE L572 MATMUL ps_a<-p,v 128*64 128x256 f32 x8 [0.61 <-DVE big L994]
...
114.19 0.39 PE L478 MATMUL ps_f<-ident,comb_rows 128*16 128x128 f32 x2 [0.28 <-DVE it L949]
...
115.74 0.39 PE L421 MATMUL ps_f<-x2h,weg_hi 128*128 128x256 f32 x1 [0.23 <-DVE it L949]
```

Values 2 start 3.31 us sooner than in after (T0+11.27 and T0+14.58). Half is given back: slot 3 is 0.91 longer, with the 0.28 and 0.23 of the rows shown, and values 6 to values 7 takes 4.72 and not 3.96: the first multiplication starts 1.6 us sooner than in after (T0+27.74 and 29.31), but values 6 are due 2.4 sooner, so p13 is late for them. The median shows none of the 1.65: 687.38 against 687.73, intervals overlapping. In the profiled execution the tail has a granted clock of 0.50 from 663 to 669 us, and from the `lg` of step 17 to the end it takes 23.6 us where after takes 20.8.

both_ends adds to it the VectorE multiplication of scale_on_dve in steps 14 and 15 alone, where GpSimd is the late one:

```diff
-                    if "F" in on and at < B and k in (5, 6, 7):
+                    if "F" in on and at < B - 2 and k in (5, 6, 7):
```

> heads_first, and in steps 14 and 15, where slots 5 to 7 wait for GpSimd, the multiplications by cb on VectorE (1.07 us each there, as the run with all of them on VectorE showed). Theory: on top of heads_first 0 to 1.7 us in step 14, according to when the spread lands, and 0 in step 15 (33.50 against 33.38 in that run): 682 to 685 us.

Step 14 takes 36.72 and not 38.32. Step 2 took 39.02, because this time its loads landed late, as GpSimd's timeline shows (T0 = 99.84):

```profile
129.30 2.53 POOL L408 TENSOR_TENSOR it<-it,cb 128x512 f32<-128x512 f32 x2 [4.85 <-DMA cb<-c_rows]
```

At 685.82, above the 682 to 685 that I expected, it is 0.3% below the kernel after, and the intervals of the two ratios overlap: not separated from it.

## Why the prediction was right or wrong

The median was forecast at 689.5 and measured 687.73; for the profiled execution 687.2 stood against 687.0. It is rival A, but the agreement to 0.2 us is luck: misses of +2.3 (step 14), +2.1 (step 2) and +0.4 (step 15) cancel others of -1.7 (start), -1.5 (steps 3 to 13) and -1.5 (tail). By the steps of the prediction:

- *Step 1, `cB` costs 0.96 a step.* Right in its new place (0.99 by pairs_back). Wrong was its reason against rival D, that the pairs stood back to back with their neighbours. So they did, and yet three of the four stood in a stretch whose length ScalarE sets (narrow_cb): a job on a busy engine is free when a wait further on would only grow by it. That all of the 0.96 is gained is due to the new order, where pairs_back found no such stretch. Work and waits were counted apart and added up; the sum held only since both go together. Also misread was whose bank `x2T` waited for: it was that of `v` 2, the first `v` of slot 7 and not the second.
- *Step 2, the waits.* The walk of the slots was within 0.15 us in six of eight; slot 4 was 0.34 longer and slot 7 0.24 shorter. New waits were 0.26 and not 0.4, all at `g` 3 as far as distances show: period 38.87 and not 39.0. The thin chain of slots 1 and 2 was a right reading: moved by a slot it costs 1.0 (newton_back), robbed of its cover 2.4 (y2_together). Relus 12 and 13 end at T0+31.6 or 1.2 into slot 6, where 1.1 stood.
- *Step 3, GpSimd.* The price was wrong, 1.28 and not 1.04, from a row with one operand stream. In steady steps it cost nothing: one_stream, at 1.04, has the same period. But it took 0.5 us of the slack of step 4. That the moved value scalings cost nothing is right.
- *Step 4, the DMAs.* The store went out as predicted (T0+17.2); the loads were issued at T0+20.2 to 22.3 (20.3) and were ready 7.0 to 8.0 us later (6.2): T0+27.5 to 29.3 and not 26.5. So the 2.6 us of slack were 0 to 1.8. The estimate in the prediction from the Trainium skill, "SBUF — State Buffer", section "Door 1: The DMA port swizzle", was 6.8 from issue and T0+27.1; its transfer time was nearer than the row of the `qk` store that I chose. It left out, as I did, that landing scatters by a microsecond and more between equal steps. Deadline and price were right within 0.2 us (spread_more), the deadline by two errors that cancel: the two multiplications before p12 take 2.53 and not 2.08, and p12 may start at T0+31.8 and not 31.2. The prediction's own sign of being wrong, a first multiplication after T0+29, came in two of the steps (29.3 in step 2, 29.1 in step 5). Rival C was about one microsecond away from deciding, and in one step each of one_stream and both_ends it did cost 0.5 and 0.8.
- *Step 6, the odd steps.* This is where the prediction failed. Step 2 was to gain 1.0 and lost 1.14. "The norm chain sticks out" was right, but I let it delay only its own readers and didn't ask who is queued in it on VectorE: `gated_heads(1)` stands within the Newton rounds, and values 1 wait for it. The fall of the clock behind the wait, 1.7 us, was not in the sum at all. Step 14 was to gain 2.5 and gained 0.21: GpSimd was charged at 1.04, and the deadline of step 4 was not moved forward in a step with shorter slots. Of the missing 2.3, spread_once gives back 1.7 (late data), and one_stream another 0.23 beyond it (dearer multiplications); 0.38 stays open.
- *Start and tail at 0.* The tail's -1.49 is a stretch at the lower clock in the profiled execution of before. The start's -1.71 lies outside the bounds of -1 and +1, and the clock does not explain it: six kernels with this start take 99.6 to 101.0 whatever their clock there. It may be the move of `v` 3; that stays open.

Rival B is refuted for steady steps (one hidden wait of 0.26), and D was right about `cB` 1 to 3 in the order before and wrong about the whole. C stayed hidden in steady steps and decided step 14.

## What to carry to other kernels

Before a job on the bound engine is counted as work that can be saved, ask whether the next job was ready: shorten the job in the old order and see whether the period follows, and look at the starts around it to see that it and the job behind it together did become shorter. Where an order is made dense for the steady step, walk the odd steps with the same care, naming for each operation moved ahead who is queued behind it when its cover is missing. A hidden transfer should be given its deadline and the scatter of its landing, not a mean: here the landing scattered by 1.8 us, and that was all of the slack.

## What the runs showed of the hardware

- A GpSimd multiplication of 128x512 takes 1040 ns with one full tensor read and 1282 ns with two.
- A VectorE multiplication of the same size with both operands in SBUF takes 0.68 us alone. Two beside GpSimd's squares took 2.13, the second of them 1.53 (scale_on_dve).
- Two broadcast loads of 512 KB to 64 partitions each were ready 7.0 to 8.0 us after issue; a 16 KB store took 3.6 us in the median and let the loads go 2.9 to 5.0 us after it (steps 2 to 14). Both scatter between steps that are alike.
- Behind stretches in which TensorE stood idle for 2 to 3 us, the granted clock was at or near 0.50 in one to three windows of 2 us in some places, and stayed at 1.00 in others with the same idle time (the tail of before and of after; the steps of y2_together). One such fall cost 1.5 to 2.8 us here (the extra 1.5 of a y2_together step; the tail of heads_first against that of after).
- A pair of matmuls narrowed from 256 to 8 columns starts its successor 0.10 us sooner, but the first matmul of 512 columns behind it then takes 0.31 us from start to start and not 0.23 (narrow_cb).
